# New orders for the heads of a cross-attention loop on TensorE, ScalarE, VectorE and SyncE

## What is computed

```python
q_hk = (hidden_q @ Wq.T).reshape(Bv, Sv, H, K)              # A
q_big = jnp.einsum('bshk,hkq->bshq', q_hk, w_kc_q)          # B
q_big = _apply_rope(q_big, sin_q[...], cos_q[...])          # rot
kv_r = _apply_rope(kv_c, sin_k[None], cos_k[None])
q_r = jnp.einsum('bshq,hqr->bhsr', q_big, W_qr)             # C
k_r = jnp.einsum('bld,hdr->bhlr', kv_r, W_kr)               # K
scores = jnp.einsum('bhsr,bhlr->bhsl', q_r, k_r)            # score
attn = jax.nn.softmax(scores, axis=-1)                      # max, exp
ctx_c = jnp.einsum('bhsl,bld->bhsd', attn, kv_r)            # V
ctx_lat = jnp.einsum('bhsd,hkd->bhsk', ctx_c, w_kc_kv)      # M, O
return ctx @ Wo.T                                           # M, O
```

## Time and profile before

| | |
|---|---|
| time, three runs | 858.93, 863.16 and 860.63 us, median 860.63 |
| span of the profiled execution | 861.5 us; nothing is recorded of what lies around it |
| PE busy | 757.3 us, 88% of the span |
| DVE busy | 766.2 us, 89% |
| ACT busy | 573.6 us, 67% |
| POOL busy | 577.6 us, 67% |

### The profile page before, as it was taken

The page is one execution under the profiler, slowest core; times in us unless marked ns, Lnnn a source line. Parts: engine busy times, 40 slices in busy tenths (PEclk is TensorE's granted clock), DMA queues, the critical chain, the costliest instruction groups (busy, mean ns, idle before and its releaser), DMA issues.

```text
span 861.5 us, 12578 instructions
## 1 busy us (share of the span) xinstructions
PE 757.3 (88%) x3268; PEld 487.1 (57%) x3268; DVE 766.2 (89%) x1026; ACT 573.6 (67%) x838; POOL 577.6 (67%) x581
## 2 busy tenths in 40 slices
PE   3678998989999999999999999999999675868996
PEld 3555565756666666666566656665666442424543
DVE  5799899989998999899989999999999767797895
ACT  2477677767766867687667766776777576774332
POOL 5769674867486757766776668576848474867462
PEclk9889999999999999999999999999999797889999
DMA  9216867776768576858676766677668999400000
GB/s 330 79 49 115 169 130 140 138 167 134 151 114 170 117 161 132 170 111 167 118 160 134 152 128 138 149 137 150 125 146 213 241 227 275 164 0 25 13 24 37
DMA packets 294405, 118.50 MB, mean 138 GB/s; under 512 B 271856, under 2 KB 278000, under 8 KB 294128
## 3 DMA queue, kind: packets, MB, share of 16 engines
q1 hardware_dynamic: 293568, 116.68, 62.0%
q10 hardware_dynamic: 816, 1.57, 0.5%
HBM read 49.02 MB, written 2.10 MB: 59 GB/s over the span
## 4 chain that ended last, share of the span: by engine, by line
PE 35%; POOL 20%; DVE 18%; issue 11%; DMA 7%; SPq 5%; ACT 3%; POOLq 1%; DVEq 0%; ACTq 0%
PE banks L1419 22%; POOL rot_cos L1055 5%; PE scores L1720 5%; DMA load<-in_pack 4%; POOL rot_lo L1063 4%; SPq L943 4%; PE scores L1507 3%; PE banks L1735 3%; DVE neg_max L1323 3%; POOL rot_hi L1061 2%; DVE rows L1330 2%; POOL rot_sin L1046 2%; DVE rot_cos L1295 2%; DVE cv_lo L1288 1%; POOL wq_lo L388 1%
## 5 line engine op out<-in xcount | busy, mean ns | idle before, releaser
L1185 ACT ACTIVATE scores<-scores,neg_max 128x1024 f32<-128x1024 f32 x128 | 139.2, 1087 | 56.1 <-DVE neg_max L1323 54.6
L1330 DVE SCALAR_TENSOR_TENSOR rows<-scores,rows 128x1024 f16<-128x1024 f32 x128 | 154.9, 1220 | 13.7 <-ACT rows L1196 12.6
L1419 PE MATMUL banks<-pt,v_hi 128*128 128x512 f16 x512 | 154.3, 383 | 12.5 <-DMA pt<-rows 11.4
L1323 DVE TENSOR_REDUCE neg_max<-scores 128x1 f32<-128x1024 f32 x128 | 155.5, 1216 | 2.9 <-PE scores L1507 2.7
L1055 POOL TENSOR_TENSOR rot_cos<-rot_cos,rot_sin 128x512 f32<-128x512 f32 x93 | 119.2, 1281 | 46.6 <-DVE rot_sin L1297 42.2
L1196 ACT ACTIVATE rows<-scores 128x1024 f16<-128x1024 f32 x128 | 130.8, 1022 | 5.2
L1063 POOL TENSOR_TENSOR rot_lo<-rot_cos,rot_hi 128x512 fp32r<-128x512 f32 x93 | 119.6, 1286 | 7.8
L1159 ACT CAST cv_hi<-banks 128x512 fp32r<-128x512 f32 x64 | 37.6, 587 | 102.6 <-PE banks L1419 101.4
L1318 DVE SCALAR_TENSOR_TENSOR acc<-banks,inv,acc 128x512 f32<-128x512 f32 x128 | 91.4, 745 | 8.0 <-PE banks L1419 4.1
L1419 PE MATMUL banks<-pt,v_lo 128*128 128x512 f16 x256 | 97.8, 382 | 0.0
L1419 PEld LDWEIGHTS banks<-pt,v_hi 128*128 128x128 f16 x512 | 44.5, 98 | 79.2 <-issue 36.4
(11 more groups left out here) (211 smaller groups left out, 1824.7 us busy)
## 6 DMA issues: line engine op xcount, KB each, us to landing
load<-in_pack SPq DMA_DIRECT2D x15, 320.0 KB, 3.5
raw_chunk<-in_out_w SPq DMA_DIRECT2D x8, 512.0 KB, 5.2
raw_chunk<-in_gate_w SPq DMA_DIRECT2D x8, 512.0 KB, 4.4
raw_chunk<-in_val_w SPq DMA_DIRECT2D x8, 512.0 KB, 4.6
raw<-in_gate_w SPq DMA_DIRECT2D x8, 512.0 KB, 5.5
raw<-in_val_w SPq DMA_DIRECT2D x8, 512.0 KB, 5.2
raw<-in_out_w SPq DMA_DIRECT2D x8, 512.0 KB, 7.0
load<-in_pack SPq DMA_DIRECT2D x15, 256.0 KB, 3.3
```

The lines of the kernel that those rows point to most:

```text
L1185: nc.scalar.activation(scores[:, u % 2, :], scores[:, u % 2, :], ACT.Exp, bias=neg_max[:, u:u + 1], accum_out=sums[:, u:u + 1]).then_inc(e ...
L1323: nc.vector.tensor_reduce(neg_max[:, u:u + 1], scores[:, u % 2, :], AX, ALU.max, negate=True).then_inc(max_ready, 1)
L1330: nc.vector.scalar_tensor_tensor(out=rows[:, u % ROWS, 1, :], in0=scores[:, u % 2, :], scalar=WEIGHT_LIFT, in1=rows[:, u % ROWS, 0, :], op ...
L1419: mm = nc.tensor.matmul(out, ws[a], xs[c], start=first and n == 0, stop=last and n == 2)
```

## The change

Eight tables are reordered: those of PE, ACT, DVE and SP, odd and even. No instruction is added, removed or altered. What moves:

- PE, odd: three of the four parts of A 0 go ahead of score tile 0. PE, even: one part of A 0 goes ahead of it, and K 1 1 behind the last part.
- PE, odd: score 2 goes from behind V 1 part 3 to behind part 6; C 0 part 2 behind B 1 1; K 0 0 behind V 0 part 4. At the ends, one O goes behind a part of C 1: in odd heads O 0 3 comes last, behind C 1 part 2.
- DVE, odd: B 0 0 and B 0 1 go ahead of low 0, O 1 2 ahead of O 1 1, low 6 behind O 0 2, and C 1 ahead of O 0 3. DVE, even: B 0 0 goes ahead of low 0, but B 0 1 behind low 1; low 2 goes ahead of O 1 1, and max 7 ahead of O 0 0.
- ACT, odd: C 1 goes ahead of exp 7, abs 0 ahead of M, double 1 ahead of exp 3. ACT, even: abs 2 goes ahead of A 1, C 0 ahead of exp 4, double 1 ahead of exp 3, and V 0 ahead of double 0.
- SP, odd: the pair goes ahead of everything, lot 3 and chunk 0 behind turn 1, chunk 1 ahead of turn 4. SP, even: chunk 0 goes behind turn 0, lot 0 ahead of turn 4.

Of the tables, the lines with the first and the third of these:

```diff
 ODD_PE = (
-    ("score", 0), part(0, 4, A0), part(1, 4, A0), part(2, 4, A0), part(3, 4, A0), ("score", 1), ("B", 0, 0, "next"),
+    part(0, 4, A0), part(1, 4, A0), part(2, 4, A0), ("score", 0), part(3, 4, A0), ("score", 1), ("B", 0, 0, "next"),
...
 EVEN_DVE = (
-    ("low", 7, "last"), ("K", 1, 0), A0, ("max", 0), ("K", 1, 1), ("max", 1), ("low", 0), ("B", 0, 0, "next"),
-    ("B", 0, 1, "next"), ("low", 1), ("max", 2), ("B", 0, 2, "next"), V1, ("max", 3), ("O", 1, 0, "last"),
+    ("low", 7, "last"), ("K", 1, 0), A0, ("max", 0), ("K", 1, 1), ("max", 1), ("B", 0, 0, "next"), ("low", 0),
+    ("low", 1), ("B", 0, 1, "next"), ("max", 2), ("B", 0, 2, "next"), V1, ("max", 3), ("O", 1, 0, "last"),
```

More of the change, by code:

```diff
@@ L102 @@
     ("high", 7, "last"), ("K", 1, 0), A0, ("K", 1, 1), ("exp", 0), ("high", 0), ("exp", 1), ("high", 1),
-    ("B", 0, 2, "next"), V1, ("exp", 2), ("high", 2), ("exp", 3), ("double", 1, "last"), ("high", 3), A1, ("abs", 2),
-    ("M",), ("exp", 4), ("high", 4), C0, ("exp", 5), ("high", 5), ("B", 1, 2, "next"), ("double", 0, "next"), V0,
+    ("B", 0, 2, "next"), V1, ("exp", 2), ("high", 2), ("double", 1, "last"), ("exp", 3), ("high", 3), ("abs", 2), A1,
+    ("M",), C0, ("exp", 4), ("high", 4), ("exp", 5), ("high", 5), ("B", 1, 2, "next"), V0, ("double", 0, "next"),
     ("exp", 6), ("high", 6), ("exp", 7), C1,
@@ L108 @@
     ("high", 7, "last"), A0, ("exp", 0), ("high", 0), ("exp", 1), ("high", 1), ("B", 0, 2, "next"), V1, ("exp", 2),
-    ("high", 2), ("exp", 3), ("high", 3), ("double", 1, "last"), A1, ("M",), ("abs", 0), ("exp", 4), C0, ("high", 4),
-    ("exp", 5), ("high", 5), ("K", 0, 0, "next"), ("K", 0, 1, "next"), ("B", 1, 2, "next"), V0, ("double", 0, "next"),
-    ("exp", 6), ("high", 6), ("abs", 1), ("exp", 7), C1,
+    ("high", 2), ("double", 1, "last"), ("exp", 3), ("high", 3), A1, ("abs", 0), ("M",), ("exp", 4), C0, ("high", 4),
@@ L112 @@
+    ("exp", 5), ("high", 5), ("K", 0, 0, "next"), ("K", 0, 1, "next"), ("B", 1, 2, "next"), V0,
+    ("double", 0, "next"), ("exp", 6), ("high", 6), ("abs", 1), C1, ("exp", 7),
 )
 EVEN_DVE = (
-    ("low", 7, "last"), ("K", 1, 0), A0, ("max", 0), ("K", 1, 1), ("max", 1), ("low", 0), ("B", 0, 0, "next"),
-    ("B", 0, 1, "next"), ("low", 1), ("max", 2), ("B", 0, 2, "next"), V1, ("max", 3), ("O", 1, 0, "last"),
-    ("O", 1, 1, "last"), ("low", 2), ("O", 1, 2, "last"), ("O", 1, 3, "last"), ("low", 3), A1, ("max", 4), ("M",),
+    ("low", 7, "last"), ("K", 1, 0), A0, ("max", 0), ("K", 1, 1), ("max", 1), ("B", 0, 0, "next"), ("low", 0),
@@ L117 @@
+    ("low", 1), ("B", 0, 1, "next"), ("max", 2), ("B", 0, 2, "next"), V1, ("max", 3), ("O", 1, 0, "last"),
+    ("low", 2), ("O", 1, 1, "last"), ("O", 1, 2, "last"), ("O", 1, 3, "last"), ("low", 3), A1, ("max", 4), ("M",),
     ("B", 1, 0, "next"), ("B", 1, 1, "next"), ("max", 5), C0, ("low", 4), ("low", 5), ("B", 1, 2, "next"), V0,
-    ("max", 6), ("O", 0, 0), ("max", 7), ("low", 6), ("O", 0, 1), ("O", 0, 2), ("O", 0, 3), C1,
+    ("max", 6), ("max", 7), ("O", 0, 0), ("low", 6), ("O", 0, 1), ("O", 0, 2), ("O", 0, 3), C1,
@@ L124 @@
+    ("O", 1, 1, "last"), ("low", 3), ("O", 1, 3, "last"), A1, ("max", 4), ("M",), ("B", 1, 0, "next"),
     ("B", 1, 1, "next"), ("max", 5), C0, ("low", 4), ("low", 5), ("K", 0, 0, "next"), ("K", 0, 1, "next"),
-    ("B", 1, 2, "next"), V0, ("max", 6), ("O", 0, 0), ("max", 7), ("O", 0, 1), ("low", 6), ("O", 0, 2), ("O", 0, 3),
-    C1,
+    ("B", 1, 2, "next"), V0, ("max", 6), ("O", 0, 0), ("max", 7), ("O", 0, 1), ("O", 0, 2), ("low", 6), C1,
+    ("O", 0, 3),
 )
@@ L208 @@
 EVEN_SP = (
[L209 to L210 removed]
+    ("turn", 7, "last"), ("lot", 2), ("lot", 3), ("turn", 0), ("chunk", 0), ("turn", 1), ("turn", 2), ("turn", 3),
+    ("lot", 0), ("turn", 4), ("turn", 5), ("turn", 6), ("lot", 1),
 )
 ODD_SP = (
[L213 to L214 removed]
+    ("pair",), ("turn", 7, "last"), ("lot", 2), ("turn", 0), ("turn", 1), ("chunk", 0), ("lot", 3), ("turn", 2),
+    ("turn", 3), ("chunk", 1), ("turn", 4), ("lot", 0), ("turn", 5), ("lot", 1), ("turn", 6),
 )
```

23 lines of the change are left out of this document (11 added, 12 removed).

## The result

The changed kernel is slower. Its median is 873.09 us (six runs, 869.25 to 875.64), that of the kernel before 861.69 us on the same chip (six runs, 858.43 to 863.66). The ratio is 1.0141, with an interval of 1.0116 to 1.0165.

A forecast was written before the change was run, and what follows sets the result against it. PE and DVE looked full, but a ring of waits through POOL was taken to set the pair's time. Six passages at 1.5 us (9.1 us) plus a last 0.8 gave 9.9 us, so 860.6 became 870.5 us, range 862 to 876.

The forecast's parts named there:

- a ring that runs through POOL: Loop of waits through DVE, POOL and PE said to set the 83.3 us pair; delays on it are paid once a pair.
- step 3: POOL, even head: idle 0.52 us before rot 1 0 absorbs delay; rot 1 0 starts 1.1 us later, released by POOL's order.
- Step 1: End of odd head, DVE and ACT: C 1 waits for ACT with O 0 3 behind it; cost 0.5 us, bounds 0 and 0.7.
- Step 2: Even head, DVE: low 1 ahead of B 0 1 delays POOL's rot 0 0; cost 1.13 us.
- rot 1 0 in even heads still waits for DVE: Sign in the changed kernel's profile, on POOL, that would show the prediction wrong; no size given.
- Step 4: SP, even head: load of `wq` issued ahead of turn 4, so POOL's w 0 waits less; gain 0.1 us.
- Step 5: Start of odd head, PE: score 0 inside A makes A to B 0 0 5.3 us instead of 4.8; cost 0.5 us.
- Step 6: PE, K 0 0 behind one more part of V 0: its 0.54 us wait goes, but no gain is taken.
- Step 7: All remaining moves: together zero; bounds a gain of 0.2 us a pair or a loss of 0.5 from late transfers.
- DVE alone sets the pace: Rival: POOL's idle time takes the delay, leaving only 0.5 us for each of 7 odd heads; 864 us, chance 0.17.
- PE sets the pace: Rival: K 0 0's wait goes, saving 0.70 us in each of 7 odd heads; 856 us, faster, chance 0.09.
- a transfer is late as well: Rival: chunk 0 or turn 7 late, one more microsecond a pair on A 1 or V 1; 877 us, chance 0.09.

The follow-up runs named there:

- d_end: Kernel before with only the changed end of the odd head on PE, ACT and DVE; pair 83.95 us, 0.63 above before.
- d_b01: Kernel before with only both low halves ahead of B 0 1 on DVE in even heads; pair 83.98 us, 0.66 above before.
- ev_sp: Kernel before with only SP's even table as changed; ratio 0.9991, pair 83.29 us.
- warm_d: d_score0 with score tile 0 computed an extra time ahead of A in odd heads; ratio 1.0020, pair 83.89 us.
- warm_after: Changed kernel with score tile 0 computed an extra time ahead of A in odd heads; 870.47 us.
- u_three: Changed kernel with the moves undone in u_b01, u_score0 and u_end all undone, other moves kept; ratio 1.0060, pair 83.78 us.
- d_sp: Kernel before with only SP's two tables as changed; ratio 1.0012, pair 83.68 us.
- u_score0: Changed kernel with score tile 0 back ahead of A on PE in odd heads; clean pairs gained only 0.1 us.
- d_score0: Kernel before with only three parts of A ahead of score tile 0 on PE in odd heads; ratio 1.0116, pair 85.37 us.
- u_b01: Changed kernel with B 0 0 and B 0 1 ahead of low 1 again on DVE in even heads; pairs without a clock fall 84.15 and 84.57 us.
- u_end: Changed kernel with the end of the odd head as before on PE, ACT and DVE; pairs without a clock fall 84.37 and 84.46 us.

## Why the prediction was right, and what it left out

The forecast was 870.5 us in a range of 862 to 876, slower. The median is 873.1. Against the kernel before the change cost 11.4 us, where 9.9 were forecast. The mechanism, a ring that runs through POOL, is what the runs show; one link of it, in step 3, works otherwise than was said. By its steps:

- **Step 1, +0.5.** Measured +0.54 in the changed kernel, +0.52 in d_end. C 1 waits 0.70 us for ACT.
- **Step 2, +1.13.** Measured +1.05, and +1.11 in d_b01.
- **Step 3, -0.52.** Measured -0.51 in both, but that the size fits is in part luck. The step said that POOL's own order would then release rot 1 0, and not DVE. It doesn't: in all even heads of the loop, in the kernel before, the changed kernel and d_b01, rot 1 0 starts 0.08 us after DVE's last product of B 1 1. In head 4 of the changed kernel that product ends at 247.23 + 0.68 = 247.91, and rot 1 0 starts at 247.99:

```profile
247.23 0.68 DVE L1297 TENSOR_TENSOR rot_sin<-banks,sin 128x512 f32<-128x512 f32 x1
```

POOL still idles 0.11 us before it. A rotary sum that waits for nothing follows without a gap, as rot 0 1 does in the same head:

```profile
235.55 1.29 POOL L1063 TENSOR_TENSOR rot_lo<-rot_cos,rot_hi 128x512 fp32r<-128x512 f32 x1
236.79 1.30 POOL L1055 TENSOR_TENSOR rot_cos<-rot_cos,rot_sin 128x512 f32<-128x512 f32 x1
```

What has changed is why DVE's product is late, and that is POOL's doing. On PE the last part of C 0 stands ahead of B 1 1 and now waits 0.46 us for `rot_lo`, and DVE's first product of B 1 1 then waits 0.59 us for PE; before, neither waited. So the delay of rot 0 0 reaches rot 1 0 by a second way, through PE and DVE, which the prediction did not have. It leaves 0.11 us of the idle time, the mean of which was 0.62. The forecast had come to the same number from the smallest idle time, 0.56, less 0.04 for a gap that isn't there: two misreadings that offset each other. By the prediction's own sign, "rot 1 0 in even heads still waits for DVE", this step came out wrong, and the time did not, since either way the delay is that of rot 0 0.

- **Step 4, -0.1.** Measured -0.20. One head had been read, with a wait of 0.13 us; over the six passages it is 0.16 on the mean. And the 0.04 that was taken off as normal isn't there: in ev_sp's head 5, with no wait, `wq_hi` starts at 256.92 and `rot_lo` ends at 255.67 + 1.28 = 256.95. ev_sp shows that the gain is real only as long as A, and not `wc`, holds B 0 0, as in the changed kernel. In the kernel before it is worth nothing.
- **Step 5, +0.5.** This is the term that was mis-sized. The new length of A to B 0 0, forecast at 5.3 us, is 5.33 in warm_d and warm_after within 0.01. But the old one was read in one passage, at 4.8, and its mean is 4.69, so the step is +0.64. And what it leaves out is PE's clock, a further 1.6 us at each fall: one in six passages of the profiled execution, +0.26 us a pair. Together +0.90. The score tile inside A costs what was said, 0.9 us: in head 5 A's fourth part begins 3.09 us after the first (261.61 to 264.70), where it was 2.17.
- **Step 6, nothing.** K 0 0's wait is gone, and u_three is not faster than d_sp. Right.
- **Step 7, nothing, with bounds of -0.2 and +0.5.** Right in the changed kernel (B 0 0 to V 1 +0.03), but only since A is late, and even so two of its six passages take 2.59 and 2.57 us there, the others 2.2 to 2.3. In d_sp, u_three and u_score0 V 1 waits for its transposes, 0.35 us a pair. It is SP's odd table that does it: ev_sp, without it, has 2.28 us there. In it the pair's loads of key weights now go out ahead of turn 7; that this move and no other of the table is the cause was not tried. So the bound was right and the place was named, but the value zero rests on a cover that another step of the change makes.

The sum: 1.60 us a pair without the clock, where 1.5 was forecast, and 1.86 with it. Six pairs make 11.1 us. The 0.8 us of the passage from head 14 to 15 can't be tested: what follows V 1 of head 13 took 255.2 us before and 255.7 after, and other kernels with the same tail spread over seven microseconds.

**The rivals.** That DVE alone sets the pace fell with d_b01 and warm_d: the first only reorders DVE's work, the second leaves DVE's table as it was and has no fall of the clock, and the pairs of both are longer, by 0.66 and 0.57 us. For a kernel with such a ring the busiest engine is not the answer: POOL, busy 58 of 83 us, sits in it. The Trainium skill ("Perfetto Trace Analysis", section "Identifying the Most-Contended Engine") has the rule that the engine of highest occupancy is the most contended. This case's traces don't agree with it, and the time by it, 864 us, is outside what was measured. That PE sets the pace fell with step 6. That a transfer is late as well was right of V 1 and the sign, and is worth 0.35 us a pair where A isn't late, not 1.

**What stays open.** Which passages see PE's clock fall. In the changed kernel it was one of six, with pauses of 0.61 and 1.21 us around two matmuls in the passage without a fall as in the one with it. I did not find what tells them apart. Nor can I say how many falls the other executions of the changed kernel had: only one was profiled, and their times range from 869.25 to 875.64 us. For d_score0 the granted clock of the whole execution speaks: 0.961 in the profiled one, with its six falls, and 0.960 to 0.961 in the other three, where the twelve of warm_d have 0.966 to 0.976. What is shown is that the falls of d_score0 go away when the pause is filled, and that a fall costs 1.6 us.

## What to carry to other kernels

Where engines walk fixed tables, write down the ring that a period closes on and price each move by the link it lies in. Busy shares didn't tell, and the same half microsecond was worth all or nothing by whether it moved one end of a slack or both. When a part is undone and the time stays, look at the links and the clock before saying that the part was free: u_b01 and u_end gained 0.58 and 0.52 us in clean pairs and lost it to the clock. And what fills a wait of PE may be worth more there than anywhere else: score tile 0 cost nothing while PE stood waiting for `wq_lo`.

## What the runs showed of the hardware that was not expected

PE's clock can fall to its lower level, 1.2 of 2.4 GHz, in the middle of a loop in which PE is busy 93% of the time (78.64 of 84.80 us). In the changed kernel it happened once in the loop, at the start of head 7:

```profile
344.44 0.51 PE L1461 MATMUL banks<-rot_hi,wr 128*128 128x512 f32 x1 [0.61 <-POOL rot_lo L1063]
...
346.38 0.80 PE L1419 MATMUL banks<-x_hi,wq_hi 128*128 128x512 f32 x1 [1.21 <-POOL wq_lo L388]
...
347.40 0.63 PE L1419 MATMUL banks<-x_hi,wq_lo 128*128 128x512 f32 x1
...
353.27 0.51 PE L1419 MATMUL banks<-cv_hi,wc_hi 128*128 128x512 f32 x1 [0.50 <-DVE cv_lo L1288]
```

and its window of four microseconds, granted clock 0.57:

```profile
346.00:350.00 4.00, 3.62 (x9) 2.91 (x10) 2.84 (x4) 1.40 (x2) 0.81 (x2) 0.57 0.86 174
```

Matmuls then follow each other at 0.43 us in place of 0.23, and A to B 0 0 takes 6.89 us (346.38 to 353.27) in place of 5.33 (261.61 to 266.94): 1.56 us for one fall. What PE did before it was to idle 0.6 us, run two matmuls in 0.7 us, and idle 1.2 us, in d_score0 1.2 to 1.5 us. In the kernel before the same place has the two matmuls, then the four of score 0, and an idle time of 0.38 us, and no fall in six passages. d_score0 fell in six of six; with the tile computed an extra time it fell in none. The Trainium skill ("TensorE: Matmul & The Clock Gate", section "A second HAM failure mode: psum-queue depth-cycling") tells of a kernel in which "the PE micro-idles between MM groups frequently enough" for the clock to go up and down. The traces here agree as far as that short idle times stood before every fall of the loop, 1.2 to 2.1 us the longest of them. They also show that such an idle time alone doesn't do it: five of the changed kernel's six passages have the 1.21 us and no fall, and single idle times of 1.28 us in d_b01 (head 2) and 1.47 us in warm_after (head 2) had none behind them.

The cost of score tile 0's move and the falls at the start of odd heads have one root, the pause that the tile used to fill: in the fourteen kernels such falls stand only where it is moved and nothing fills its place. The tile was charged twice, once for its 0.9 us inside A, and once for the clock that its absence let fall.
